# Four weight loads issued after the first stage, a Square moved from ScalarE to VectorE, and a multiplication moved from VectorE to GpSimd, in a windowed-attention and feed-forward layer on eight cores

## What is computed

```
q = x @ Wq + bq            # 16 heads of 64
k = x @ Wk + bk            # 2 key/value heads of 64, 8 query heads share one
v = x @ Wv + bv
kp, vp = pad(k, 128 on both sides), pad(v, ...)
scores[s, w] = q[s] . kp[s + w],  w in 0..255        # no scaling
probs  = softmax(scores over w)
attn   = (sum over w of probs * vp[s + w]) @ Wo + bo
y      = layernorm(x + attn)

y_prev = y shifted by one position
xr = mu_r * y + (1 - mu_r) * y_prev
xk = mu_k * y + (1 - mu_k) * y_prev
r  = sigmoid(xr @ W_r.T)
k2 = square(relu(xk @ W_k.T))
out = layernorm(y + r * (k2 @ W_v.T))
```

## Time and profile before

| | |
|---|---|
| time, median of 2 runs | 1098.39 us (1096.81 to 1099.98) |
| the profiled execution's own time | 1097.3 us |
| its span, slowest core (core 5) | 1095.8 us (other cores 1083.2 to 1093.5) |
| TensorE busy | 583.0 us (53%) |
| VectorE busy | 301.6 us (28%) |
| ScalarE busy | 283.9 us (26%) |
| GpSimd busy | 21.5 us (2%) |
| mean granted TensorE clock, share of full speed | 0.732 |

### The profile page before, as it was taken

The page is one execution under the profiler, slowest core; times in us unless marked ns, Lnnn a source line. Parts: engine busy times, 40 slices in busy tenths (PEclk is TensorE's granted clock), DMA queues, the critical chain, the costliest instruction groups (busy, mean ns, idle before and its releaser), DMA issues. The chain is left out here.

```text
span 1095.8 us, 11430 instructions; the slowest of 8 cores (1083.2 to 1095.8 us)
## 1 busy us (share of the span) xinstructions
PE 583.0 (53%) x2834; PEld 223.9 (20%) x2834; DVE 301.6 (28%) x765; ACT 283.9 (26%) x754; POOL 21.5 (2%) x37
## 2 busy tenths in 40 slices
PE   0045567674566655565655555653095195293392
PEld 0012222221122211121211112221042042141141
DVE  0011122122222222222222221222504615515524
ACT  0000111444334234333324333321022132132032
POOL 2000000000000000000000000000000000000000
PEclk9998788755666556666656666656599598598697
DMA  9999892232322332232323323341230211201001
GB/s 117 155 110 159 150 173 39 54 72 64 62 65 63 61 75 63 62 63 65 76 57 74 67 56 70 63 73 29 51 45 39 60 27 58 64 4 58 20 1 77
DMA packets 178143, 75.06 MB, mean 68 GB/s; under 512 B 165920, under 2 KB 166048, under 8 KB 178080
## 3 DMA queue, kind: packets, MB, share of 16 engines
q1 hardware_dynamic: 165248, 48.37, 23.0%
q0 software_dynamic: 12832, 25.96, 13.0%
HBM read 43.01 MB, written 8.39 MB: 47 GB/s over the span
## 5 line engine op out<-in xcount | busy, mean ns | idle before, releaser
L497 ACT ACTIVATE p<-psc,konst 128x384 bf16<-128x384 f32 x272 | 155.9, 577 | 313.9 <-PE psc L485 303.3
L565 PE MATMUL po<-pt,vt 128*64 128x128 bf16 x408 | 63.6, 290 | 179.0 <-DMA pt<-p16n 179.0
L855 PE MATMUL pr<-w16r,xr 128*128 128x512 bf16 x256 | 63.4, 414 | 127.4 <-DVE xk L834 127.4
L479 PE MATMUL psc<-maskq,ident 128*128 128x384 bf16 x272 | 106.5, 426 | 35.5 <-ACT p L497 30.1
L602 PE MATMUL pwo<-w16o,ao 128*128 128x512 bf16 x272 | 99.9, 534 | 22.4 <-DVE ao L585 22.4
L585 DVE CAST ao<-po 128x512 bf16<-128x512 f32 x34 | 23.5, 692 | 208.0 <-PE po L570 208.0
L565 PEld LDWEIGHTS po<-pt,vt 128*64 128x64 bf16 x408 | 36.0, 141 | 214.7 <-issue 214.7
L300 PE MATMUL paP<-xfm,w16k 128*128 128x512 bf16 x40 | 17.6, 618 | 113.1 <-DMA xfm<-x16t 113.1
L524 DVE TENSOR_SCALAR p16n<-p,rall 128x384 bf16<-128x384 bf16 x272 | 65.3, 309 | 0.2 <-issue 0.2
L570 PE MATMUL po<-pt,vt 128*64 128x128 bf16 x408 | 65.1, 293 | 0.0
L918 PE MATMUL pr<-w16vf,kact 128*128 128x512 bf16 x256 | 56.5, 379 | 12.7 <-DVE kact L899 6.6
(11 more groups left out here) (68 smaller groups left out, 500.1 us busy)
## 6 DMA issues: line engine op xcount, KB each, us to landing
x<-xpad POOLq DMA_DIRECT2D x17, 512.0 KB, 3.8
out<-out SPq DMA_DIRECT2D x16, 512.0 KB, 2.6
x16t<-xpad POOLq DMA_DIRECT2D x5, 1024.0 KB, 11.2
pt<-p16n SPq DMA_TRANSPOSE x136, 2.8
w16q<-wq POOLq DMA_DIRECT2D x1, 2048.0 KB, 32.3
w16o<-wo POOLq DMA_DIRECT2D x1, 2048.0 KB, 55.9
w16r<-wr POOLq DMA_DIRECT2D x1, 2048.0 KB, 23.1
w16kf<-wkf POOLq DMA_DIRECT2D x1, 2048.0 KB, 22.5
```

What stands on the lines that cost most here:

```text
L479: e.matmul(psc[:, HH % 3, 0:WIN], ident[:, :], maskq[:, :], start=True, stop=False)
L497: e.activation(p16[:, tau % 2, h, :], psc[:, H % 3, 0:WIN], AF.Exp, bias=konst[:, 0:1], accum_out=sall[:, h:h + 1]).then_inc(bEX.sem, 1)
L565: last = e.matmul(po[0:64, slot * 128:(slot + 1) * 128], lhs, pt16[:, slot_a, c * 128:(c + 1) * 128], start=(c == 0), stop=(c == 2), tile_ ...
L855: last = e.matmul(pr[:, pru % 2, nh * 512:(nh + 1) * 512], xr16[:, kc, ts * 128:(ts + 1) * 128], w16r[:, kc, nh * 512:(nh + 1) * 512], sta ...
```

## The change

Four edits. First, the four late weights are no longer loaded during stage A: they are issued by POOL at the start of stage B's block, ahead of the first load of `x32`. Second, the sum of squares of the first layernorm is computed by VectorE with a multiplication instead of by ScalarE's Square. Third, each chunk of the mixing in stage C gets one more wait, on VectorE's own previous result. Fourth, the squaring of `krelu` goes from VectorE to GpSimd.

```diff
             load_xbatch(g)
             load_xbatch(g + 1)
-            if wlate:
-                nm, wt, win_ = wlate.pop(0)
-                v_wlate[nm] = g_dma(wt[:, :, :],
-                                    win_.ap().rearrange("(c p) n -> p c n", p=128))
...
+        wlate_defer = []
         while wlate:
             nm, wt, win_ = wlate.pop(0)
-            v_wlate[nm] = g_dma(wt[:, :, :],
-                                win_.ap().rearrange("(c p) n -> p c n", p=128))
+            ch = Chan(nc, chst, "gw_%s" % nm)
+            ch.post(16)
+            def fw(e, d=wt, s=win_, ch=ch):
+                e.dma_start(d[:, :, :],
+                            s.ap().rearrange("(c p) n -> p c n", p=128)) \
+                    .then_inc(ch.sem, 16)
+            wlate_defer.append(fw)
+            v_wlate[nm] = ch.tok()
...
             sch.emit(_eng, lambda e: wtok(e, v_ident, v_maskq, aVT_final))
+        for fw in wlate_defer:
+            sch.emit("gpsimd", fw)
...
             def fsq(e, vz=vz):
                 e.wait_ge(bZ.sem, vz)
-                e.activation(sqd[:, :], z32[:, :], AF.Square,
-                             accum_out=lnt[:, 1:2]).then_inc(bSQ.sem, 1)
-            ln_s.emit("scalar", fsq)
+                e.scalar_tensor_tensor(sqd[:, :], z32[:, :], 1.0, z32[:, :],
+                                       ALU.mult, ALU.mult,
+                                       accum_out=lnt[:, 1:2]).then_inc(bSQ.sem, 1)
+            ln_s.emit("vector", fsq)
...
                     dsync = sfV.post()
+                    e.wait_ge(sfV.sem, dsync - 1)
                     e.tensor_sub(d16[:, :], yfm[:, chx, 16:528],
...
-                tail.emit("vector", fka)
+                tail.emit("gpsimd", fka)
```

## The result

The changed kernel took 1106.05 us (median of 11 executions, 1102.48 to 1109.22); the kernel before, run beside it, took 1097.52 us (median of 10, 1092.92 to 1109.25). The ratio is 1.0083, with a 95% interval of 1.0064 to 1.0102: slower by some 9 us, within the 2% that the forecast called "no change". The forecast was 1104 us.

What follows compares the result with a forecast made beforehand. PE waits for transposes; in stage B a serial chain from z to the scaling sets the turn. 1097.3 - 13 + 37 - 31 + 12 + 1 = 1103, as a measured time 1104 us; range 1075 to 1127.

Steps and rivals of the forecast that it cites:

- no change: Whole kernel: a measured time within about 2%, from 1076 to 1120 us; chance 0.61.
- Stage A: Start of stage A: without the late weights the first transposes finish sooner and PE starts near 58 us; -13 us (-7 to -16).
- The loads: Start of stage B: four weight loads slow the transposes, z of tile 0 at 78 us into the stage; +37 us.
- Fair shares: Start of stage B: transposes keep their pace beside weights, z waits only for x32; +22 instead of +37, 1089 us; chance 0.15.
- Square: Stage B's turns: Square on DVE lets Ln start 2.08 us sooner in 15 layernorms; -31 us (-28 to -34).
- The rival in which the move does nothing: Stage B: transposes or PE set the turn, so moving the Square gains 0; 1134 us; chance 0.05.
- the clock's in stage B: Stage B: the shorter stall keeps the clock up, mean 0.75 not 0.64, PE's time shrinks by 47; 1056 us; chance 0.06.
- Squaring on GpSimd: Stage C: squaring krelu takes 1.25 us on GpSimd, so ACT and POOL set the pace; +12 us (0 to +36).
- The added wait: Stage C's mixing: 32 already satisfied waits for xr at 0 to 0.06 us each; +1 us (0 to 2).

Runs made afterwards that it cites:

- e6: Kernel before with Square on DVE, w16o, w16r and w16kf in stage A's groups 1 to 3, w16vf behind tile 0's x32; 1053.46 us, ratio 0.9633.
- e5: Kernel before with only the four late weights moved to the start of stage B, behind x32 of tiles 0 and 1; 1115.21 us, ratio 1.0201.
- e9: Kernel before with the sum of squares moved to DVE and the multiplication done twice; 1067.97 us, ratio 0.9787.
- e2: Kernel before with only the sum of squares moved from ACT's Square to DVE; 1061.95 us, ratio 0.9738.
- e3: Kernel before with only the squaring of krelu moved from DVE to GpSimd; 1104.89 us, ratio 1.0123.
- e7: Kernel before with the squaring of krelu on GpSimd and a second krelu buffer; 1100.00 us, ratio 1.0061.

## Why the prediction was right, and where its steps were not

The time of 1104 us was met by 1106 because the two large terms and stage A were about right, and not because nothing happened. In stage C it was in part luck: the duration was too high, and a term was missing.

*Stage A, forecast -13, measured -14.* The step held: transposes freed of `w16o` were to end 12.3 us sooner, and from the first transposes to PE it is 12.1 us less (24.8 to 12.7, means of the cores). The start of PE was put near 58 us and was 53.8 because I counted from 45.33, where the first transposes began on one core of one execution; on the core read now they began at 41.46, and from there it took 12.3 us, for the 12.7 assumed. The miss in the mark is the spread between cores. The later groups gave 0.6 us, for the 1 taken. That nearly the whole gain belongs to `w16o`, e6 shows.

*The loads, forecast +37, measured +35.* The end of the load was forecast at 58 us into the stage and was 58.5; z of tile 0 at 78, and it was 77.4. Three pairs were through and not two: a transpose did take 15.9 to 27.9 us to land (19 was forecast), but two or more were in flight at once, and PE got one every 10.3 to 10.5 us. It made little difference, since behind the load the fourth still waited 6.15 us. By e5, `x32` is no limit. Fair shares is refuted by z at 77 us instead of 63: q1 had 9.9% of the engines and q0 92.5%. By the Trainium skill, DMA: Bandwidth & Descriptors, "Queues, rings and completion order", the engines alternate between queues packet by packet; q1's 3009 packets for 0.75 MB (250 bytes each) against q0's 4251 for 8.76 MB (2060 bytes each) don't contradict turns of one packet each, but equal turns are no equal time, and a transpose is not protected by them.

*Square, forecast -31, measured -28.* The chain was read rightly to the last link: Ln stands behind the exponentials in the kernel after, PE's stall is 5.20 us where 5.3 was forecast, and e9 confirms that even twice the multiplication is hidden. The size was 1.9 us per turn and not 2.08. PE's stall did shrink by 2.1 us in most turns (7.27 to 5.16), so the rest of a turn has grown by 0.2, and no view says where. The rival in which the move does nothing is refuted by e2, as is the clock's in stage B: its granted clock is 0.64 after as before. Stage B of the kernel after, as in the earlier trace rows:

```profile
189.68:749.40 559.72, 317.05 (x1666) 108.79 (x1666) 155.46 (x489) 175.37 (x577) 12.53 (x21) 0.64 0.40 80
```

*Squaring on GpSimd, forecast +12, measured +13.6 in e3, with half of it for another reason.* The squaring takes 1.04 us and not the 1.25 chosen; the ratio of two engines' smallest fills overstates it. By the Trainium skill, GPSIMD Engine Reference, "Elementwise — side-by-side cycle accounting", the estimate was 1.1 us, and the trace roughly agrees with its 1.04 us. With 1.04 the step that I summed gives 7 x 0.14 + 0.62 = 1.6 us per group, +6.4 in all, and that part was measured at 6.5. The others, 6.7 us in e3 and 4.5 in the kernel after as means of the cores, are PE's matmuls at the lower clock; on the four cores of the kernel after where it fell they are 8.9 us, and these cores tell in a time that is the slowest core's. The forecast had a rival about the clock, but in stage B, where it is low anyway; it asked nowhere what a longer pause does to a stretch that runs at 1.00. An error of 6 us in the duration and a missing term of about that size cancelled, by luck. Of the 16.3 us in stage C of the kernel after, 6.5 (chain), 3.4 (wait) and 4.5 (clock) are accounted for; 2 us are not.

*The added wait, forecast +1 (0 to 2), measured +3.4.* The step "`xk` was waited for already, so another satisfied wait costs 0 to 0.06 us" failed: it costs about 0.07 us in the step itself by the timeline, 0.1 by stage C's length.

The sum of the forecast was +6 on a profiled execution of 1097.3 us, and the timed difference is 8.5. That the total is so close rests on errors of 2 to 6 us with both signs.

## What to carry to other kernels

A bulk load that nothing needs yet is still priced by the short transfers that are due while it runs: put it where no serial chain hangs on a small transpose. The same two megabytes cost 13 to 14 us beside the first transposes, 8 in a turn, 1 to 2 at the start of stage B and nothing measurable in stage C. A step that moves to a slower engine can be priced twice, by its own chain and by what the pause before the next dense stretch does to TensorE's clock; look at all cores for the second, since the slowest one alone overstates how often it happens. And take a change apart before judging it: here three edits that cost 2.2, 1.2 and 0.35% hid one that gains 2.6%, and keeping one weight out of the first group's way gained another 1%.

## What the runs showed of the hardware that was not expected

- Behind a longer pause of PE ahead of a dense stretch of stage C the granted clock often falls, and not always. The product of 48 matmuls took 10.52 us behind pauses of 1.6 us in every group of every core, and 12.1 to 13.4 us in 28 of 32 groups (e3) and 16 of 32 (after) behind 3.25 us, and in 18 of 32 behind 2.3 us (e7). In the first group of core 7 it still reads 1.00 at the product's start (811 to 813 us) and 0.64 from 813 to 815; in the third it reads 0.70 within the pause (977 to 978).
- DMA transposes of 192 KB beside a weight load that converts to bfloat16 land after 15.9 to 27.9 us in the kernel after, where the median of the whole run is 2.8 (transposes of the tile `pt`, issued from 195 to 225 us):

```profile
DMA to landing us min/median/max: 15.9/25.1/27.9
```

- GpSimd's bfloat16 multiplication of 128x512 takes 1.04 us to DVE's 0.42, and passing a tile from ACT to POOL and back adds only 0.14 and 0.09 us: from 808.81, the end of the piece that starts at 808.21, to 808.95, and from 809.99 to 810.08.
- A wait for a semaphore that was reached 0.8 us before costs DVE something: the pause ahead of the subtraction reads 0.17 us on each of 28 chunks, and the steps are 0.07 us longer.
